# Transfers of 123 to 127 partitions issued as two: partitions 0 to 111, and the rest

## The reference: what is computed

```
xn = layernorm(x)
x  = x + gnn_0(xn, src, dst)       + mix_0(xn)     # 8 heads, softmax over the edges of a node
x  = x + ffn_0(layernorm(x))                       # 16 experts, top 2
xn = layernorm(x)
x  = x + gnn_1(xn, type, weight)   + mix_1(xn)     # one weight matrix for each of 8 relations
x  = x + ffn_1(layernorm(x))                       # 8 experts, top 1, capacity 489
xn = layernorm(x)
x  = x + gnn_2(xn, weight)         + mix_2(xn)     # sum over edges, two batch norms
x  = x + ffn_2(layernorm(x))                       # 8 experts, top 2, width 1024
xn = layernorm(x)
x  = x + gnn_3(xn)                 + mix_3(xn)     # attention over source nodes
x  = x + ffn_3(layernorm(x))                       # one expert, half of the rows chosen
```

## Time and profile before

| | |
|---|---|
| time of three runs, median | 6609.47 us |
| the profiled execution, its span | 7077.1 us |
| PE busy | 4218.2 us, 60% of the span |
| DVE busy | 3514.2 us, 50% |
| POOL busy | 2994.4 us, 42% |
| ACT busy | 1880.9 us, 27% |
| hardware queue q1 | 236.85 MB, 10.3% of 16 DMA engines |
| software queue q0 | 359.47 MB, 21.0% |

### The profile page before, as it was taken

The page is one execution under the profiler, slowest core; times in us unless marked ns, Lnnn a source line. Parts: engine busy times, 40 slices in busy tenths (PEclk is TensorE's granted clock), DMA queues, the critical chain, the costliest instruction groups (busy, mean ns, idle before and its releaser), DMA issues. The chain is left out here.

```text
span 7077.1 us, 68012 instructions
## 1 busy us (share of the span) xinstructions
PE 4218.2 (60%) x17738; PEld 2957.9 (42%) x17738; DVE 3514.2 (50%) x8546; ACT 1880.9 (27%) x4929; POOL 2994.4 (42%) x3029
## 2 busy tenths in 40 slices
PE   0023467777777397376666591455444994577659
PEld 0001334444444375134444481334324884355436
DVE  6900478888888512535554204553244112555447
ACT  0000046666666121003343120000011221244321
POOL 0677023333333155116666361666601443366520
PEclk9985688888888698688877695777676997798879
DMA  1001023333334175133336231333612663233220
GB/s 39 3 15 26 12 75 98 101 98 97 97 99 89 47 212 168 67 142 89 91 91 85 69 96 50 96 92 93 86 18 66 188 190 113 80 89 88 78 43 19
DMA packets 361123, 600.60 MB, mean 85 GB/s; under 512 B 119026, under 2 KB 245091, under 8 KB 357371
## 3 DMA queue, kind: packets, MB, share of 16 engines
q0 software_dynamic: 162496, 359.47, 21.0%
q1 hardware_dynamic: 198256, 236.85, 10.3%
HBM read 517.26 MB, written 78.63 MB: 84 GB/s over the span
## 5 line engine op out<-in xcount | busy, mean ns | idle before, releaser
L1665 POOL DMA_INDIRECT g0e_got<-g_table,g0e_rc x496 | 475.3, 958 | 1072.2 <-DVEq L1825 729.0
L1418 POOL DMA_INDIRECT g1e_got<-g_table,g1e_rc x496 | 489.1, 986 | 526.2 <-DMA g1e_rc<-rec_dst 294.0
L1418 POOL DMA_INDIRECT g2e_got<-g_table,g2e_rc x496 | 479.3, 966 | 338.8 <-issue 140.4
L1418 POOL DMA_INDIRECT g3e_got<-g_table,g3e_rc x440 | 429.2, 975 | 361.9 <-issue 116.3
L1474 PE MATMUL g2e_pa<-g2e_got,g2e_placew 128*125 128x256 f32 x992 | 338.6, 503 | 380.5 <-DVEq L1576 259.3
L250 POOL DMA_INDIRECT rec_dst<-bydst_rc,bydst_sloti x391 | 398.6, 1019 | 300.6 <-DVEq L442 175.4
L2628 PE MATMUL f_p<-f_w2s,f_hid 128*128 128x256 f32 (+1 forms) x2176 | 498.9, 386 | 40.8 <-ACT f_hid L2648 28.2
L1753 PE MATMUL g0e_spread<-g0e_expanded,g0e_by_tile 128*125 128x512 bf16 x992 | 414.5, 507 | 180.4 <-ACT g0e_spaced L1702 144.5
L2617 PE MATMUL f_p<-f_xt,f_w1s 128*128 128x256 f32 (+1 forms) x2176 | 495.4, 385 | 18.8 <-issue 6.7
L1702 ACT ACTIVATE g0e_spaced<-g0e_spread 125x512 bf16<-125x512 f32 x992 | 499.4, 624 | 20.7 <-remote 6.8
L2648 ACT ACTIVATE f_hid<-f_p,f_b1s 128x256 f32<-128x256 f32 (+1 forms) x544 | 251.7, 472 | 854.7 <-PE f_p L2617 480.7
(11 more groups left out here) (656 smaller groups left out, 8236.5 us busy)
## 6 DMA issues: line engine op xcount, KB each, us to landing
f_w1s<-in_L_ffn_W SPq DMA_DIRECT2D x32, 1024.0 KB
f_w2s<-in_L_ffn_W SPq DMA_DIRECT2D x32, 1024.0 KB
g_table<-g1t_out SPq DMA_DIRECT2D x25, 1000.0 KB
f_w1s<-in_L_ffn_w SPq DMA_DIRECT2D x40, 512.0 KB
f_w2s<-in_L_ffn_w SPq DMA_DIRECT2D x40, 512.0 KB
f_results<-f_y SPq DMA_DIRECT2D x72, 256.0 KB
f_b2s<-in_L_ffn_b SPq DMA_DIRECT2D x80, 128.0 KB
f_rows<-XN SPq DMA_DIRECT2D x3, 3125.0 KB
```

What stands on the lines that cost most here:

```text
L1418: pool.indirect_dma_start(got[:, g % GOTS, j, :], None, table, bass.IndirectOffsetOnAxis(rc[:, g * GT + j, idx:idx + 1], 0))\
L1665: pool.indirect_dma_start(got[:, s, j, :], None, table, bass.IndirectOffsetOnAxis(rc[:, sl, j, R_IDX:R_IDX + 1], 0)).then_inc(got_in[s], 16)
```

## The change

`spans(rows)` gives two slices of partitions, 0 to 111 and 112 to the end. Each transfer at the lines named above is issued once for each slice, in place of once for all partitions. Every completion adds 16 to the same semaphore as before, so all waits on these counts are doubled (48 in place of 32 in the sort, where the transfer of the last partition stays one). The bytes, their places and their order are the same. The result stores of f0 and f2 have 128 partitions and go through the same helper as those of f1 with 123, so they are also issued as two, of 112 and 16.

```diff
--- before.py
+++ after.py
@@ -48,6 +48,12 @@
 MEM = 4
 CHUNK = 4 * P
 NCH = N // CHUNK
+SPREAD = 112
+
+
+def spans(rows):
+
+    return (slice(0, SPREAD), slice(SPREAD, rows))
 
 
 class Resident:
@@ -184,9 +190,10 @@
 
         @block.sync
         def _(sp):
-            sp.dma_start(R.X[:, :].rearrange("p (t d) -> p t d", d=D),
-                         x.rearrange("(t p) d -> p t d", p=P)).then_inc(x_loaded, 16)
-            sp.wait_ge(x_loaded, 16)
+            for own in spans(P):
+                sp.dma_start(R.X[own, :].rearrange("p (t d) -> p t d", d=D),
+                             x.rearrange("(t p) d -> p t d", p=P)[own, :, :]).then_inc(x_loaded, 16)
+            sp.wait_ge(x_loaded, 32)
 
         @block.gpsimd
         def _(pool):
@@ -295,7 +302,8 @@
             for b in sorts:
                 sp.wait_ge(b.padded, 1)
                 for to, of in b.inputs():
-                    sp.dma_start(to[0:127, :], of[0:127 * EC].rearrange("(p c) -> p c", c=EC)).then_inc(b.loaded, 16)
+                    for own in spans(127):
+                        sp.dma_start(to[own, :], of[0:127 * EC].rearrange("(p c) -> p c", c=EC)[own, :]).then_inc(b.loaded, 16)
                     sp.dma_start(to[127:128, 0:TAIL], of[127 * EC:E].rearrange("(p c) -> p c", p=1)).then_inc(b.loaded, 16)
 
             sp.wait_ge(made_empty, 1)
@@ -348,7 +356,7 @@
             for n, b in enumerate(sorts):
                 rcf = b.rc[:, :, :].bitcast(F32)
                 loc = rcf[:, :, b.loc]
-                dve.wait_ge(b.loaded, 32 * len(b.inputs()))
+                dve.wait_ge(b.loaded, 48 * len(b.inputs()))
                 dve.tensor_copy(b.kf[:, :], b.ki[:, :])
                 dve.tensor_copy(b.rc[:, :, R_IDX], b.gi[:, :])
                 if b.relation is not None:
@@ -548,9 +556,10 @@
             if store is not None:
                 for t in range(NT):
                     sp.wait_ge(finished, t + 1)
-                    sp.dma_start(store(t), out[:, t % OUTS, :]).then_inc(stored[t % OUTS], 16)
+                    for own in spans(P):
+                        sp.dma_start(store(t)[own, :], out[own, t % OUTS, :]).then_inc(stored[t % OUTS], 16)
                 for k in range(OUTS):
-                    sp.wait_ge(stored[k], 16 * len(range(k, NT, OUTS)))
+                    sp.wait_ge(stored[k], 32 * len(range(k, NT, OUTS)))
 
         @block.scalar
         def _(act):
@@ -607,7 +616,7 @@
             for t in range(NT):
                 dve.wait_ge(multiplied, t + 1)
                 if store is not None and t >= OUTS:
-                    dve.wait_ge(stored[t % OUTS], 16 * (t // OUTS))
+                    dve.wait_ge(stored[t % OUTS], 32 * (t // OUTS))
                 finish(dve, t, ps[t % OUTS], out[:, t % OUTS, :] if store is not None else None)
                 dve.drain().then_inc(finished, 1)
 
@@ -2436,9 +2445,10 @@
 
         @block.sync
         def _(sp):
-            sp.dma_start(rows.rearrange("(t p) d -> p t d", p=P),
-                         R.XN[:, :].rearrange("p (t d) -> p t d", d=D)).then_inc(kept, 16)
-            sp.wait_ge(kept, 16)
+            for own in spans(P):
+                sp.dma_start(rows.rearrange("(t p) d -> p t d", p=P)[own, :, :],
+                             R.XN[own, :].rearrange("p (t d) -> p t d", d=D)).then_inc(kept, 16)
+            sp.wait_ge(kept, 32)
 
         @block.gpsimd
         def _(pool):
@@ -2569,10 +2579,11 @@
                     if s % each == 0 and s // each + 1 < NE:
                         load(s // each + 1)
                     sp.wait_ge(taken, (s + 1) * TJ)
-                    sp.dma_start(results[s * TS:(s + 1) * TS, :].rearrange("(j p) d -> p j d", p=RP),
-                                 y[:, s % 2, :, :]).then_inc(stored[s % 2], 16)
+                    for own in spans(RP):
+                        sp.dma_start(results[s * TS:(s + 1) * TS, :].rearrange("(j p) d -> p j d", p=RP)[own, :, :],
+                                     y[own, s % 2, :, :]).then_inc(stored[s % 2], 16)
                 for k in range(2):
-                    sp.wait_ge(stored[k], 16 * len(range(k, NS, 2)))
+                    sp.wait_ge(stored[k], 32 * len(range(k, NS, 2)))
 
             @block.gpsimd
             def _(pool):
@@ -2669,7 +2680,7 @@
                     k, wk = s % 2, weights_of(s)
                     dve.wait_ge(w_in[wk], weights_in(s))
                     if s >= 2:
-                        dve.wait_ge(stored[k], 16 * (s // 2))
+                        dve.wait_ge(stored[k], 32 * (s // 2))
                     for j in range(TJ):
                         n = s * TJ + j
                         dve.wait_ge(second, n + 1)
@@ -2924,9 +2935,10 @@
                     sp.dma_start(w[:, q, :, r * D:(r + 1) * D], chunks_of(W[2 * q + r], D)).then_inc(loaded[q], 16)
             for t in range(NT):
                 sp.wait_ge(taken, (t + 1) * PAIRS)
-                sp.dma_start(to[t * P:(t + 1) * P, :], out[:, t % 2, :]).then_inc(stored[t % 2], 16)
+                for own in spans(P):
+                    sp.dma_start(to[t * P:(t + 1) * P, :][own, :], out[own, t % 2, :]).then_inc(stored[t % 2], 16)
             for k in range(2):
-                sp.wait_ge(stored[k], 16 * len(range(k, NT, 2)))
+                sp.wait_ge(stored[k], 32 * len(range(k, NT, 2)))
 
         @block.tensor
         def _(pe):
@@ -2946,7 +2958,7 @@
         def _(dve):
             for t in range(NT):
                 if t >= 2:
-                    dve.wait_ge(stored[t % 2], 16 * (t // 2))
+                    dve.wait_ge(stored[t % 2], 32 * (t // 2))
                 for q in range(PAIRS):
                     n = t * PAIRS + q
                     dve.wait_ge(multiplied, n + 1)
@@ -3139,9 +3151,10 @@
     with nc.Block() as block:
         @block.sync
         def _(sp):
-            sp.dma_start(table.rearrange("(t p) d -> p t d", p=P),
-                         src[:, :].rearrange("p (t d) -> p t d", d=D)).then_inc(stored, 16)
-            sp.wait_ge(stored, 16)
+            for own in spans(P):
+                sp.dma_start(table.rearrange("(t p) d -> p t d", p=P)[own, :, :],
+                             src[own, :].rearrange("p (t d) -> p t d", d=D)).then_inc(stored, 16)
+            sp.wait_ge(stored, 32)
 
 
 def isomorphism_graph_layer(nc, R, a, by_dst):
@@ -3439,10 +3452,11 @@
                 rows = out.rearrange("(t p) d -> p t d", p=P)
                 for q, (at, tiles) in enumerate(chunk):
                     sp.wait_ge(summed, q + 1)
-                    sp.dma_start(rows[:, 4 * q:4 * q + tiles, :],
-                                 R.X[:, 4 * q * D:(4 * q + tiles) * D].rearrange("p (t d) -> p t d", d=D))\
-                        .then_inc(stored, 16)
-                sp.wait_ge(stored, 16 * NQ)
+                    for own in spans(P):
+                        sp.dma_start(rows[own, 4 * q:4 * q + tiles, :],
+                                     R.X[own, 4 * q * D:(4 * q + tiles) * D].rearrange("p (t d) -> p t d", d=D))\
+                            .then_inc(stored, 16)
+                sp.wait_ge(stored, 32 * NQ)
 
 
 def fourth_feed_forward(nc, R, a, out):
```

## The result

The changed kernel takes 6509.23 us, median of 4 runs (6505.12 to 6514.46), against 6608.74 us for the kernel before (4 runs beside it). The ratio is 0.985, 95% interval 0.9836 to 0.9864, so 99.5 us or 1.5% are gained. Forecast were 6498 us and 111 us.

The account below looks back on a forecast made before the run. No engine is busy throughout, so time is a sum of stages, with transfers slowed by poorly spread partitions. Terms 52.4 + 25.2 + 12.7 + 24 + 5 - 8 = 111 us off 6609.47 gave 6498 us, range 6450 to 6545.

Parts of the forecast that it names:

- Engines by divisors: All touched transfers: the number of engines divides the number of partitions, so 112 should run on all sixteen.
- rival (a): Split transfers: parts don't run beside each other, or the first doesn't spread; nothing gained, 6617 us; chance 0.03.
- Whole-table transfer: x, f1 dispatch and row store: each falls from about 28 us to 10.8, together saving 52.4 us.
- f0 and f2 dispatch: Dispatch stages, uncovered only in part: save 5.6 and 7.1 us, then DVE's chain of comparisons is late next.
- Sort: Sort's loads of 127 partitions: DVE's whole wait for them goes, 25.2 us.
- Relation tables: Relation-table stores: PE paces each tile at 6.88 us, and the end shortens by 6.5 us; 24 us saved.
- Small store ends: Last stores of f1, the two row-stage tables and the output: 5 us saved, bounds 2 and 7.
- First table stage: First layer's table stage (g0qv): gain taken at nothing, since its second tile idles on DVE without a store to wait for.
- rival (c): First table stage meets its stores unprofiled, 25 us more, and f0's cost is nothing, 8 us: 6465 us; chance 0.16.
- Second issue in f0: f0 experts: second store issue delays the next expert's weights in about 20 tiles, costing 8 us, bounds 0 and 16.
- Rival (d): Expert loops of f0 and f2: SP becomes the bound; at 3 us per tile, 6707 us; chance 0.02.
- Rival (b): Spreading at its bad end: whole table 18 us, only the relation tables' end, f0 loses 16: 6546 us; chance 0.13.

Follow-up runs that it names:

- the odd execution: The kernel before, unchanged, in the one profiled execution the prediction was read from: span 7077.1 us; profiled again, 6614.1 us.

## Why the prediction was right, and where it was not

The sum held in sign and nearly in size, 111 us against 99.5. The parts, tried alone, add up by their medians: tables 49, sort 25, relation tables 25, row stages 0, the second issue of 128 partitions -6, together 93, and about 4 us for the end of the f1 experts, seen in profiles only.

- **Engines by divisors: right.** 112 partitions run on all engines, 115 on five, 13 on thirteen, by the 4-byte packets. The cut at 115 separates this from "two parts", and rival (a) is out: the first part does spread, though the second does start late, as (a) has it.
- **Whole-table transfer, 10.8 us: the term that was mis-sized.** It measured 17.0 us for x and 14.1 and 14.0 for the stores, and that is 6.1, 2.9 and 2.8 us less gained, 11.8 us, where the forecast is off by 11.5. Two steps failed. The first is "they are nothing beside the rest", of the 13 partitions. They do spread over 13 engines, as assumed there, but they come behind the large part and leave a tail of 3.2 us at x and 3.3 and 3.2 at the stores. At the two stores that is the whole shortfall. The second is "At 381 GB/s the bytes take 8.4 us", at x: the rate came from the clearing of a 128-partition table, and while x is loaded the 112 partitions move at 249 to 294 GB/s, which is the other 3 us. The stores reach 323 GB/s. The doubt stood there ("could also be less for rows of 1 KB"), with 16 to 18 us as the bad end. The size of the rows alone is not the cause, since 1 KB rows move at 102 or more than 182 GB/s by which partitions they are. The sum itself was also 0.2 to 0.4 us low: 8.4, 2.0 and two issues of 0.3 to 0.4 are 11.0 to 11.2.
- **f0 and f2 dispatch, 12.7 us: right**, 13.0. DVE's chain took over, so the slower transfer cost nothing here, as the prediction said of a transfer of 18 us.
- **Sort, 25.2 us: right**, 25.8 in the profile and 25 timed. It held even with 115 of the 127 partitions on five engines.
- **Relation tables, 24 us: right**, 24.6, and by its own steps: 6.87 us for each tile and 5.4 us at the end.
- **Small store ends, 5 us: about right, but not by its parts.** f1's experts end 3.8 us earlier. The two row stages alone gain nothing, and from the first issue of the f2 experts to the end of the kernel both profiles differ by 0.8 us, the output included.
- **First table stage, "I take at nothing": the right number for the wrong reason, by luck.** The step "Whatever paces it, the stores don't" was read from the odd execution. In an ordinary one DVE waits 23.5 us there for its stores, as rival (c) has it, and the change takes that away. Rival (c) is wrong in the next step: the 19.5 us are given back, since POOL's scatter ends later than the mixer. What I left out was to ask who ends the stretch that the stage stands in, though the scatter beside it was named.
- **Second issue in f0, 8 us: right in place**, 7 us alone, with a wide interval. Rival (d) is out: 72 tiles cost 7 us, not 216.

Rival (b), with 18 us for a whole table, was near for x; for the stores it was as far off as the forecast, and it was wrong on the relation tables and on f0.

## What to carry to other kernels

Look at the DMA share in sixteenths: the transfers at 0.34 and 0.07 in a bare wait were those whose number of partitions has a poor divisor, and cutting them at 112, a multiple of 16, is worth 1.5% here without touching an engine's work. Count the remainder as time of its own, 3 us here, not as nothing. Leave transfers of 128 alone: they gain no engine, and the second issue stands ahead of whatever SP issues next. Before counting a gain in one stage, find what ends the stretch it lies in, and when the profile's own time is far from the timed ones, take another profile before reading which wait comes last.

## What the runs showed of the hardware that I had not expected

- The number of engines can be read without an estimate: each transfer ends with one 4-byte packet for every engine that worked on it, 5 for x in one piece, 29 for 112 and 13 partitions, 11 for 110 and 15 for 120.
- A second transfer on SP's queue is held up at its issue behind a large one. The pair took 5.08 us behind 2800 KB on sixteen engines, when a third of the packets had started, and 21.07 us behind 2875 KB on five, when four fifths had. In both some 120 packets were left for each engine, and 86 to 89 in four stores. With 325 KB ahead, 25 packets for each engine, it took 0.77 to 0.96 us.
- With the same number of partitions, rows and bytes, a read into neighbouring partitions is slower than one into spread partitions: 5.74 us against 3.99 for 13 of them. Whether the partitions or the HBM rows that go with them make the difference is not shown. The issues with a stride took 0.70 to 0.96 us, those without 0.31 to 0.33, except 0.63 for 64 partitions.
- More engines need not be faster: 64 partitions on sixteen engines took 10.28 us, and 63 spread ones on nine took 10.47. 120 on fifteen took 18.9 us, where 112 on sixteen took 13.54. Busy engines at 120 GB/s, as beside the small part, are engines that wait.
